# Two-layer transformer kernel: expert tiles listed in two parts and interleaved from the first slot of the last turn, expert output biases added at the tiles, twelve first units, results four deep

## The reference

```python
x = x + attn0(xn) + ffn0(xn)                      # xn = layernorm(x)
# layer 1, on xn = layernorm(x):
gates = softmax(relu(xf @ Wr1 + br1) @ Wr2 + br2)
tg, ti = top_k(gates, 2);  tg = softmax(tg / 2)
out = silu(xf @ Ws1 + bs1) @ Ws2 + bs2            # shared expert
for e in range(8):
    h = silu(xf @ We1[e] + be1[e]) @ We2[e] + be2[e]
    out = out + sum(tg * (ti == e))[:, None] * h
x = x + attn1(xn) + out
```

## Time and profile before

| | us |
|---|---|
| median of 3 runs | 1429.02 (1424.39 to 1443.83) |
| the profiled execution | 1434.63 |
| its span, first to last instruction | 1432.9 |
| busy: PE, DVE, ACT, POOL | 1155.4, 934.5, 797.5, 459.0 |
| granted TensorE clock, mean | 0.920 of full |

### The profile page before, as it was taken

One profiled execution on the slowest core, in us unless ns is written; L12 is line 12 of the kernel. 1 busy time (PEld: TensorE's weight loads), 2 busy tenths in 40 slices (PEclk: granted clock), 3 DMA queues, 4 the chain that ended last, 5 costly groups with the idle time before them and its releaser, 6 DMA issues.

```text
span 1432.9 us, 19562 instructions
## 1 busy us (share of the span) xinstructions
PE 1155.4 (81%) x6807; PEld 520.0 (36%) x6807; DVE 934.5 (65%) x1600; ACT 797.5 (56%) x1077; POOL 459.0 (32%) x409
## 2 busy tenths in 40 slices
PE   2679667988898888888888988898889737888994
PEld 1212313422342343234323432243233125787841
DVE  6857747778777877877787768777872435532323
ACT  1344446476766667675767476657576402233373
POOL 9541352135224332223323333321421201344420
PEclk9667789999999999999999999899999759999997
DMA  5512073107411731261146204610510372456644
GB/s 154 117 61 57 11 198 115 34 1 193 129 34 37 189 97 34 84 189 49 35 118 172 58 9 133 174 36 7 152 34 1 95 185 85 142 174 183 182 139 124
DMA packets 149508, 144.13 MB, mean 101 GB/s; under 512 B 13689, under 2 KB 141890, under 8 KB 149410
## 3 DMA queue, kind: packets, MB, share of 16 engines
q1 hardware_dynamic: 143922, 132.96, 34.5%
q0 software_dynamic: 4544, 9.38, 2.0%
q10 hardware_dynamic: 944, 0.54, 0.1%
HBM read 90.19 MB, written 52.12 MB: 99 GB/s over the span
## 4 chain that ended last, share of the span: by engine, by line
PE 38%; DVE 16%; ACT 15%; DMA 9%; issue 7%; DVEq 6%; SPq 4%; POOL 3%; ACTq 0%; POOLq 0%
DVE nm L1054 8%; PE sums L387 8%; PE mx L399 7%; ACT ex L768 6%; PE mx L368 4%; ACT L746 4%; PE mx L489 3%; PE mx L498 3%; DMA ks<-xsort 2%; PE ring L473 2%; PE ring L289 2%; DMA scratch<-parts 2%; PE ring L299 2%; PE ring L294 2%; PE ring L356 1%
## 5 line engine op out<-in xcount | busy, mean ns | idle before, releaser
L768 ACT ACTIVATE ex<-mx 128x1024 f32<-128x1024 f32 x512 | 511.9, 1023 | 332.2 <-PE mx L399 331.6
L1054 DVE TENSOR_REDUCE nm<-mx 128x2 f32<-128x1024 f32 x512 | 600.6, 1216 | 133.9 <-PE mx L368 133.2
L399 PE MATMUL mx<-qs,ks 128*128 128x512 bf16 (+1 forms) x1024 | 312.9, 401 | 53.4 <-ACT hs L759 13.3
L387 PE MATMUL sums<-ex,vs 128*18 128x512 f32 x2048 | 297.3, 636 | 3.2 <-ACT ex L768 1.3
L399 PEld LDWEIGHTS mx<-qs,ks 128*128 128x128 bf16 (+1 forms) x1024 | 77.1, 99 | 341.9 <-issue 144.0
L368 PE MATMUL mx<-km,qm 32*128 32x512 bf16 x1024 | 149.6, 410 | 63.7 <-DVE nm L1054 38.1
L368 PEld LDWEIGHTS mx<-km,qm 32*128 32x128 bf16 x1024 | 37.9, 92 | 218.8 <-issue 84.4
L1470 POOL TENSOR_SCALAR binade<-binade 128x704 f32<-128x704 f32 (+1 forms) x24 | 56.3, 2347 | 188.7 <-DVE binade L1005 188.7
L1495 POOL DMA_INDIRECT xsort<-xn,pos_i x64 | 62.6, 978 | 169.0 <-DVE pos_i L1141 151.7
L1462 POOL TENSOR_TENSOR parts<-qk_f,parts 128x512 bf16<-128x512 f32 x32 | 36.9, 1174 | 181.7 <-DVE parts L973 181.7
L1433 POOL TENSOR_TENSOR rstd<-veps,minus_half 128x4 f32<-128x4 f32 x16 | 16.7, 1045 | 210.0 <-DVE veps L964 210.0
(11 more groups left out here) (212 smaller groups left out, 1568.3 us busy)
## 6 DMA issues: line engine op xcount, KB each, us to landing
scratch<-parts SPq DMA_DIRECT2D x128, 256.0 KB, 3.6
ks<-scratch SPq DMA_DIRECT2D x64, 256.0 KB
qs<-scratch SPq DMA_DIRECT2D x64, 256.0 KB
qs<-wmoe SPq DMA_DIRECT2D x20, 514.0 KB, 3.6
ks<-wmoe SPq DMA_DIRECT2D x19, 514.0 KB, 3.7
qm<-scratch SPq DMA_DIRECT2D x64, 128.0 KB, 2.6
km<-scratch SPq DMA_DIRECT2D x64, 128.0 KB, 2.6
rest<-parts SPq DMA_DIRECT2D x32, 128.0 KB, 3.3
```

The costliest lines, as they stand in the source:

```text
L387: done = pe.matmul(acc[32 * j:32 * j + 2 * VW, :], values[:, start:start + 2 * VW], ex[:, s % NEX, j, :], start=q == 0 and t == 0, stop=q ...
L399: done = pe.matmul(bank[:, j, :], ks[l][r, h, t * P:(t + 1) * P], qs[l][r, h, :], start=True, stop=True)
L768: act.activation(ex[:, s % NEX, 2 * i:2 * i + 2, :], bank[:, :, :], ACT.Exp, scale=SCALE).then_inc(free, 1)
L1054: dve.tensor_reduce(nm[l][:, t, h:h + 2], bank[:, :, :], AX.X, ALU.max, negate=True).then_inc(free, 1)
```

## The change

1. **Tiles in two lists.** `tile_table(part)`. Part 0 runs at (0, "a") of turn b(7), from the counts of seven batches, and lists NFULL = 21 tiles that are full for certain. Part 1 lists the other 18, at (12, "a"), after `router_weights`, where the whole table stood at (11, "b"). FIRST_TILE is 0. SP fetches tiles 0 and 1 before it stores and loads q and k of layer 1's batch 7; the clearing stands before tile 4, the second half of the stacks (`load_stacks(1, 7, 1)`) before tile 8, base and first rows before tile 12, the second rows before tile 21. For each tile weights come first, then tokens.
2. **Biases.** The weights' rows carry be2, copied to all 128 rows (1156 numbers); DVE adds it when it reads a tile's output out. bs2 is added once to the attention's bias on POOL. `w9`, its transposes, the ninth-row products and ACT's copy are gone. A weights buffer is free when DVE has read the output, not when PE has written it.
3. **First units** 12, and units of batch 1 from slot 6 of a(0) (before: from 8); the first `max_rows` one unit earlier; batch 0's silu without table loads of its own.
4. **Places.** Second `max_rows` from (1, "a") to (0, "d"); in turn a `v1` to (8, "d"), q0 and k0 of batch 2 to slots 5 and 6; in turn b `k1` to (10, "d") and the split of q and k to (11, "m"). `quantize_h` of half 1 at (1, "m"), (2, "m"), (2, "c"), (5, "m"), and its waits for POOL moved from step 0 to the steps that write what POOL reads. On POOL `third_part` changes places with `round_h`.
5. **Results** in four buffers instead of two; SP loads y of four batches before it waits.

```diff
-FIRST_TILE = 6
-FIRST_UNITS = 10
+FIRST_TILE = 0
+FIRST_UNITS, FIRST_NEXT = 12, 6
+NFULL = -(-(2 * (B - 1) * T - E * (TS - 1)) // TS)
-WROW = FE + EC * P + EC
-NW = 4
+WROW = FE + EC * P + EC + P
+NW, NRES = 4, 4
...
-                    done = pe.matmul(bank[:, t * P:(t + 1) * P], w9T[:, t * P:(t + 1) * P], b2_sb[:, :], start=False, stop=True)
...
-                    if at == (1 if b else 6, "a"):
+                    if at == ((0, "d") if b else (SLOTS - FIRST_UNITS, "a")):
                         max_rows(0, b, 1)
...
             def gates(b, i):
-                load_table(ACT.Silu, 8 * b + 2 * i)
+                if b >= 1:
+                    load_table(ACT.Silu, 8 * b + 2 * i)
...
                 if step == 0:
-                    wait(dve, xq_ready, b + 1)
-                    wait(dve, h_ready, 2 * b + i)
                     dve.drain()
                     quantize_maxima(h, 2 * F0)
                 if step == 1:
+                    wait(dve, xq_ready, b + 1)
                     quantize_scales(2 * F0, qsc[i])
...
                 if step == 3:
+                    wait(dve, h_ready, 2 * b + i)
                     quantize_binades(h, 2 * F0, binade[:, :]).then_inc(h_scaled, 1)
...
-                dve.tensor_copy(yo[i % 2], bank[:, 0, 0:TS]).then_inc(free, 1)
+                bias = wbuf[i % NW][:, WROW - P:WROW]
+                dve.tensor_tensor(yo[i % 2].rearrange("p (h c) -> p h c", c=P), bank[:, 0, 0:TS].rearrange("p (h c) -> p h c", c=P),
+                                  bias.unsqueeze(1).broadcast_to([P, 2, P]), ALU.add).then_inc(free, 1)
...
                 if i >= NW:
-                    p, before = pairs.at(("TO", i - NW))
-                    sp.wait_ge(mx_full[p], before + 1)
+                    pair_read(sp, ("TO", i - NW))
...
+                if b == LAST:
+                    sp.wait_ge(tiles_ready, 1)
+                    fetch_weights(0)
+                    sp.wait_ge(scattered, 16 * 8 * LAST)
+                    fetch_tokens(0)
+                    fetch_weights(1)
+                    fetch_tokens(1)
                 store_early(1, b)
...
+            for i in range(2, NTILE):
                 if i == 4:
+                    sp.wait_ge(ends_ready, 1)
+                    for e in range(E):
+                        clear_behind(e)
+                if i == 8:
+                    load_stacks(1, LAST, 1)
+                if i == 12:
                     store_base(LAST - 1)
                     load_rows(1, LAST, 0)
-                if i == 12:
+                if i == NFULL - 1:
+                    sp.wait_ge(tiles_ready, 2)
+                if i == NFULL:
                     load_rows(1, LAST, 1)
+                    sp.wait_ge(zero_out, 16 * E)
+                    sp.wait_ge(scattered, 16 * 8 * B)
+                fetch_weights(i)
                 fetch_tokens(i)
```

More of the change, by code:

```diff
@@ L1167, in tile_table @@
                 dve.drain()
+                if part == 1:
+                    dve.tensor_tensor(tiles[:, :], tiles[:, :], taken[:, :], ALU.subtract)
+                    dve.drain()
                 dve.tensor_tensor_scan(ends[:, :], one8[:, :], tiles[:, :], 0.0, ALU.mult, ALU.add)
                 dve.drain()
-                dve.tensor_tensor(after[:, :, :], each(iota_t), over(ends), ALU.is_ge)
-                dve.drain()
-                dve.tensor_reduce(t_exp[:, :], after[:, :, :], AX.X, ALU.add)
@@ L1173, in tile_table @@
-                dve.tensor_tensor(used[:, :, :], after[:, :, :], over(tiles), ALU.mult)
+                dve.tensor_tensor(behind, number.unsqueeze(2).broadcast_to([P, n, E]), over(ends), ALU.is_ge)
+                if part == 0:
+                    dve.tensor_tensor(begins[:, :], ends[:, :], tiles[:, :], ALU.subtract)
+                    dve.memset(skip[:, :], 0.0)
+                    dve.drain()
+                    dve.tensor_scalar(begins[:, :], begins[:, :], -1.0, float(NFULL), ALU.mult, ALU.add)
+                    dve.drain()
+                    dve.tensor_scalar(begins[:, :], begins[:, :], 0.0, None, ALU.max)
+                    dve.drain()
+                    dve.tensor_tensor(taken[:, :], begins[:, :], tiles[:, :], ALU.min)
+                    dve.drain()
+                    dve.tensor_tensor(skip[:, 0:E - 1], taken[:, 1:E], taken[:, 0:E - 1], ALU.subtract)
@@ L1174, in tile_table @@
+                dve.drain()
+                if part == 1:
+                    dve.tensor_tensor(tiles[:, :], tiles[:, :], skip[:, :], ALU.subtract)
+                    dve.drain()
+                dve.tensor_reduce(expert, behind, AX.X, ALU.add)
+                dve.tensor_tensor(steps, behind, over(tiles), ALU.mult)
                 dve.drain()
-                dve.tensor_scalar(t_exp[:, :], t_exp[:, :], float(E - 1), None, ALU.min)
-                dve.tensor_reduce(t_row[:, :], used[:, :, :], AX.X, ALU.add)
+                dve.tensor_scalar(expert, expert, float(E - 1), None, ALU.min)
@@ L1177, in tile_table @@
+                dve.tensor_reduce(row, steps, AX.X, ALU.add)
                 dve.drain()
[L1178 to L1179 removed]
+                dve.tensor_tensor(row, number, row, ALU.subtract)
+                dve.tensor_scalar(w_row[:, columns], expert, float(P), None, ALU.mult)
                 dve.drain()
[L1181 removed]
+                if part == 1:
+                    dve.tensor_scalar(row, row, taken[:, 0:1], None, ALU.add)
+                    dve.drain()
```

215 lines of the change are left out of this document (103 added, 112 removed).

## The result

The changed kernel takes 1352.8 us (median of four runs, 1350.8 to 1354.7) where the kernel before takes 1432.1 (four runs, 1424.4 to 1443.8): a ratio of 0.944 with a 95% interval of 0.937 to 0.951. The forecast was 1371 in a range of 1349 to 1399, "faster". The direction was right and the time lies in the range, 4 us above its lower end; by size it is the case C of the rivals (1352), outside the main case's own 1358 to 1385. That it meets the number of C is partly luck: of C's two parts one came true (the clock) and one did not (a tile cycle near 4.3), and other terms made up the difference. The profiled execution has a span of 1351.4 us where that of before has 1432.9, and a mean clock of 0.957 where it was 0.920.

What follows compares the result with a forecast made beforehand. Limits were taken to be nearly full PE slots, an empty stretch behind DMAs, and the tile cycle. Terms -5 - 8 - 21 - 8 - 16 - 5 = -63 from 1434.6 gave 1371 us, range 1349 to 1399.

Steps and rivals of the forecast that it cites:

- case C: Rival: no more PE holes at turn starts, clock stays 2.4 GHz (6 x 1.5), tile cycle near 4.3 (-10): 1352; chance 0.12.
- main case: The whole kernel as summed, 1371 us, with its own range 1358 to 1385; chance 0.53.
- Start: Start and turn a(0): -5 us from earlier first scores (-2.7), the wait at 105.5 gone (-2.0) and lighter slots; bounds 0, -9.
- Turn a(1): PE's 10.9 us wait for `nm_hl` goes, a later wait of 2.5 to 3 comes: -8 us; bounds -3 and -11.
- Turns a and b: Bias work and short `nm_hl` waits go: 7 x 3.0 = -21 and 6 x 1.3 = -8 us; -26 over the twelve stretches.
- Rival B: Turns keep their length as PE waits for ACT's exponentials; four fifths of 29 us lost: 1395; chance 0.13.
- To tile 2: Last turn: tile 2's tokens land at about 1161.5; -1.8 to its first unit, -23.7 from there to tile 2's transposes.
- The tiles: 39 tile steps to the last output: 4.55 us each plus slots' own work, 196 us in all, +6.5.
- rival A: Interleaved tiles run slower as PSUM pairs wait for readers: 5.0 us a tile, +17, 1388; chance 0.15.
- Rival D: Weights, now ahead of tokens in one queue, delay each tile: 7.2 us a tile, +103, 1474; chance 0.03.
- The clearing at nothing: SP's clearing of 8.4 us before tile 4 costs nothing unless SP comes to it later than 1161.
- The end: After the tiles: with four result buffers DVE begins `rden` at 1410.4 instead of 1415.34: -5 us; bounds 0 and -6.

Runs made afterwards that it cites:

- a_quant: Changed kernel with `quantize_h` of half 1 back at its old places and its waits for POOL back in step 0: 1357.8 us.
- a_places: Changed kernel with second `max_rows` back at (1, "a") and `quantize_h` of half 1 at its old places with its waits in step 0: 1385.5 us.
- a_maxrows: Changed kernel with the second `max_rows` of each turn back at (1, "a"): 1375.1 us.
- b_now9: Kernel before without `w9`, its transposes, ACT's copy and the ninth-row products, so its output lacks those biases: 1405.7 us, ratio 0.980.
- a_first6: Changed kernel with PE's tile steps starting at slot 6 of the last turn (FIRST_TILE = 6), all else kept: 1359.0 us.
- a_tok1st: Changed kernel with SP fetching each tile's tokens before its weights in the loop over the tiles: 1330.9 us.
- the five traces: Traces with second `max_rows` at (1, "a"): the kernel before in two profiles, b_now9, a_maxrows and a_places.
- a_nres2: Changed kernel with two result buffers instead of four and SP's old order at the end: 1360.4 us.

## Why the prediction was right, and where it was off

The forecast of a faster kernel rests on steps that the traces show: shorter turns without the bias work and the waits, no hole in turn a(1), and tiles that start early. Most terms held in kind; the largest miss is a term left out of the sum though it stood among the rivals.

**Start, -9.0 for -5.** The direction was right, the reasons in part. The first scores moved from 74.73 to 72.34, near my 72. I gave the two units and the wait at 105.5 most of the gain. The run with ten units has nearly all of it: with ten, its first scores come at 68.62, 6.1 us before those of the kernel before, which also had ten. So the two units are not what shortens the start, but something that both kernels share. One such thing was in no term of mine: with `quantize_h` of half 1 at its old places (a_quant) the start takes 166.9 us where the changed kernel has 160.6 and the kernel before 169.5, so 6.3 of the 9.0 hang on it. Silu without table loads and the earlier `max_rows` come ahead of the first scores; they were not run apart. The wait of 2.0 at 105.5 did go: ahead of the corresponding scores there is none with twelve units, and 1.81 (at 97.32) with ten. The bound of -9 was reached.

**Turn a(1), -10.2 for -8.** The mechanism held, and a_places shows it by bringing the wait back. My step named both causes (step 0 no longer waits, and it comes after `max_rows`) and took them as one; each is enough. The 2.5 to 3 us that I held back for the next unit's operands are not there: between 172 and 206 us PE is never idle for over 1.2. In a_maxrows this wait is there, 2.04 us at 176.97.

**Turns a and b, -42.2 for -26.** This is the term that was mis-sized. At equal clock the sum holds. The first kind of stretch gains 3.95 at a clock of 1.00 (67.93 to 63.98). The second kind, from b to a, gains 0.8 from b(1) to a(2) (66.71 to 65.88) and nothing from b(4) to a(5) (66.52 in both), all at 1.00. That is 4.0 to 4.8 a pair, and 4.3 was forecast. The remaining 16 us are stretches of before at a lower clock. They were in the rival C, at 9 us (6 x 1.5), and should have been in the sum: the mean clock of 0.920 on the page, and stretches of equal work between 67.9 and 71.8 us in the trace of before, could be seen ahead of the result. C's reason was right for part of it: PE's holes at the starts of turns are followed by a lower clock at six of twelve starts in the trace of before and at none after. The other half of the low time lies elsewhere. Rival B (ACT takes the time back) is refuted by the clean stretches and by b_now9.

**To tile 2, -28.7 for -25.5 with the turn's end.** The terms held: the last turn's first unit at 1074.28 and tile 2's transposes 19.7 us behind it, where I had 20.0. But I misread a row: the transposes at 1204.83, which wait 7.3 us, are those of tile 4. Tile 2's stand at 1183.99 in the trace of before, without a wait:

```profile
1183.99 0.44 PE L481 MATMUL ring<-ident,qs 128*128 128x128 f32 x2
```

The sum did not rest on it, since it was taken between the two ends of the tiles, 1373.5 and 1357.5; the sentence that PE waited for tile 2 until 1204.8 is wrong. And the gain comes less from PE's order than from the rest: a_first6 keeps all but 6 us.

**The tiles, +12.2 for +6.5.** 201.7 us for my 196. The step of tiles 20 to 38 is 4.77 where I had 4.55. I took 4.2 from one cycle of the chain; over tiles 20 to 38 the kernel before takes 4.32. With that the forecast step would have been 4.67. The added 0.35 itself is nearly right as a sum (4.77 - 4.32 = 0.45), but not in its parts: the wait for DVE's read is 0.31 a tile (4.77 against 4.46), and the width's 0.1 is not seen apart from the scatter. The mean step stayed under rival A's 5.0. Rival D is refuted, and its premise was wrong: the weights did not come to stand ahead of the tokens, they stood there before. That order does cost part of a step, as a_tok1st shows by 22 us, but through the wait and not through the bytes, and the sum had it in both kernels.

The read of a tile's output, priced at no more than the copy, is in the trace of the changed kernel beside a copy of the same size:

```profile
1204.32 0.42 DVE L1213 TENSOR_TENSOR qs<-mx,ks 128x256 f32<-128x256 f32 x1 [2.31 <-PE mx L494]
1206.19 0.42 DVE L1201 COPY ks<-ring 128x256 f32<-128x256 f32 x1 [1.44 <-PE ring L477]
```

Both take 0.42. The bound of the Trainium skill's page "VectorE: DVE Perf Modes", which would have allowed the copy twice the rate of the addition, does not show for float32 out of PSUM. The section "Why PSUM operands drop a tier" of the same page of the Trainium skill says as much, with 1x for fp32, and the trace agrees. The fit of 2 us plus bytes that the prediction took for the wider rows from the Trainium skill's "DMA: Bandwidth & Descriptors" is given there for DMAs issued from GpSimd, and SP issues these; the sum did not use it.

**The clearing at nothing: wrong by about 3 to 6 us.** I had named the point from which it would cost (SP coming to it later than 1161, which is 1093.8 in the changed kernel's time, counted from the last turn's first unit, forecast at 1141.5 and measured at 1074.28). SP came to it at 1093.66, on the point itself, and ended at 1102.0, and tile 4's tokens were issued at 1103.99, for transposes that PE could have begun at 1104.4; the wait of 3.33 at 1107.76 follows. The transfer behind it was forgotten in the margin.

**The end, -3.6 for -5.** DVE's last combine and its division in the changed kernel:

```profile
1332.55 2.35 DVE L1234 SCALAR_TENSOR_TENSOR macc<-ks,tg,macc 128x128 f32<-128x128 f32 x8
1334.82 0.35 DVE L1054 RECIPROCAL rden<-ring 128x32 f32<-128x32 f32 x1
```

PE's transposes end at 1334.28, and the division starts 0.5 us later, as forecast. With two buffers the end takes 2.9 more. That DVE is late was right; it still is, behind its last combine.

**What stays open.** Why the clock falls behind one wait of 1.3 or 1.4 us and not behind the next (28 of 60 in the five traces), and what makes the dips elsewhere. The long ones of the kernel before come at the same two places in two profiles and not in b_now9, but a_nres2 has two of 3.8 us with nothing changed in them. The other places of the change (q0, k0, v1, k1, POOL's order, and the waits of `quantize_x`, the rounding of the layer norm, which were moved like those of `quantize_h`) were not run apart. The twelve stretches gained 42.2; b_now9 has 19.0 of it and the two places run here 13.1 (792.4 in a_places against 779.3). If these add, the other 10 us are theirs or the clock's.

## What to carry to other kernels

In a queue that issues several transfers in turn, ask of each what it waits for, and put those that can go early ahead of those that wait for the later event; a cycle in the chain of waits that runs through such a queue is a matter of order first, and of bytes only when the rate does not rise after it. When stretches of equal work differ in length and clock, take the clean one as the price of the work, and put the difference to the others into the sum as a term of its own. A short wait of PE in a full stretch can cost more than its length: look at what stands just ahead of each fall of the clock, in more than one trace. A transfer or an issue costed at nothing needs a margin that holds its whole latency, not its issue alone.

## What I had not expected of the hardware

Sixteen-slot stretches with the same instructions took 63.98 us at a granted clock of 1.00 and 67.74 at 0.90, in two kernels that do not differ up to there. Behind waits of PE of 1.3 or 1.4 us at the starts of turns the clock fell to 1.2 GHz within 2.1 us in 28 of 60 cases, and at the same starts without the wait in none of 108. With PE busy 67.00 of 67 us, the DMA engines moved 231 GB/s beside it at a share of 0.75, so the 180 GB/s of the tile cycle were not their limit. A tensor_tensor and a copy of 128x256 float32 from PSUM took 0.42 us each.
